# TensorE computes the two score pairs of an attention unit apart, with the unit's other matmuls between them

## The chip, the cores and the metric

The kernel runs on one core of one Trainium2 chip. Times are device microseconds (us) of one execution. The figure for a kernel is the median of several runs; the profile is one execution taken apart by the hardware profiler. TensorE does the matmuls and transposes, ScalarE the exponentials and the gelu, VectorE most copies out of PSUM and the normalisations, GpSimd the gathers and some subtractions, SyncE starts the plain DMAs.

## The reference: one layer of a small language model

A batch of 8 sequences of 1024 tokens, 192 channels wide. Token rows, segment rows and positions are added; then comes attention with 12 heads of 16 channels, then a quantised feed-forward block:

```python
h = tok_table[x] + seg_table[mask] + pos
a = layernorm(h)
q, k, v = split(a @ qkv_weight.T)              # 12 heads of 16 channels
q, k = layer_norm(q) * 16 ** -0.5, layer_norm(k)
h = h + (softmax(q @ k.T) @ v) @ proj_weight.T
f = quantise(layernorm(h))
h = h + (quantise(clip(gelu(f @ w1.T + b1))) @ w2.T + b2)
```

The scores of one sequence are 12 x 1024 x 1024 numbers, each of which needs an exponential.

## The kernel before, in words

**Half-steps and units.** The work is cut into 16 half-steps, one for 512 queries of a sequence. A half-step has 24 units (`UNITS`): one unit is four heads (`GH`) by 128 keys by 512 queries. For a unit TensorE makes four score matmuls (`scores`, line 1212), each 64 rows deep and 512 columns wide, into the four PSUM banks of `ps_s`, one head a bank. Heads 0 and 1 are pair 0, heads 2 and 3 are pair 1; two heads of a pair lie in different halves of the rows. ScalarE takes each pair out with one exponential of 128x1024 into `probs` (`exps`, line 679). Later TensorE multiplies the probabilities with the values (`heads`, line 1232): four heads side by side in 32 columns each, fp32, which the profile shows as eight matmul records, summed in the one bank `ps_o` over the units of a group.

**Order on TensorE.** The order of every engine is written out by hand. `PLAN` (line 77) has one line per unit, `START_PLAN` (line 128) the same for half-step 0. A word is a job: `h` is one `heads`; A to I, X, Y and W are the other matmuls and transposes (A transposes the normed rows, B and C make q, k and v, D and E transpose q and k, F and G turn the attention output, H is the projection, I transposes the quantised rows, X and Y are the feed-forward matmuls, W turns the feed-forward weights and runs in half-step 1 alone). Small letters and N, P, R, S are VectorE work or copies that ScalarE makes. Jobs belong to other half-steps than the scores (`LAG`, line 175): those of A to E are for the half-step two ahead, so half-steps 14 and 15 have none of them.

`one` (line 1328) walks a half-step: for each unit first all four scores, then the jobs of that unit's line. `HEADS_BEHIND` (line 165) is 2: the n-th `h` of a half-step is the `heads` of unit n - 2. Counted through `PLAN` this means that unit 14's line makes `heads` of unit 13, unit 15's those of 14, unit 16's those of 15. Unit 0's line makes those of units 22 and 23 of the half-step before and unit 13's those of units 10, 11 and 12; in all others `heads` is two or three units behind. In half-step 0 `h` of units 1 to 6 is the `heads` of the unit just before.

The semaphores that matter here are these. Pair p of unit u is computed after pair p of unit u - 1 has been read by ScalarE, and `heads` of a unit waits for both exponentials of it:

```python
pe.wait_ge(exp_done, 2 * UNITS * s + (2 * u - 1 + j // 2))     # L1224, scores, at j = 0 and j = 2
pe.wait_ge(exp_done, 2 * UNITS * s + (2 * u + 2))              # L1245, heads
act.wait_ge(scores_mm, 2 * UNITS * s + (2 * u + pair + 1))     # L681, exps
```

The jobs use the three banks of `ps_j` in turn (X two of them, B the third), and wait at line 1259 for the copy of the bank's last user. On ScalarE the six gelus of a half-step (line 676) stand between the exponentials of unit 12 and unit 13, with a table load before and after them. X of block t waits for the gelu of block t - 2.

The lines of `PLAN` with what TensorE does in them, for half-steps from 2 on:

```
u0  h h          u6  h            u12 C0 B0 X0                    u18 h C2 D1
u1  Y0 Y1 Y2 F0 Y3 F1   u7  h     u13 X1 B1 X2 X3 B2 X4 X5 B3 h h h   u19 E1 h
u2  G0 F2 F3 H0 G1      u8  h I0  u14 h                           u20 D2 h
u3  h h          u9  I1 h A0      u15 h                           u21 h D3 E2
u4  G2 G3 H1 H2 H3      u10 I2 h A1 A2   u16 h                    u22 E3 h
u5  h h          u11 h A3 I3      u17 D0 E0 C1                    u23 C3 h
```

Of the kernel before, what the change touches and what calls it, by code (L numbers as in the profile page):

```python
# [27 lines left out]
X = mybir.AxisListType.X  # L28

P = 128  # L30
B, SEQ = 8, 1024
C = 192
H, D = 12, 16
# [11 lines left out]
GH = 4  # L45
# [4 lines left out]
UNITS = HG * TB  # L50
# [52 lines left out]


JOB_KINDS = "ABCDEFGHIWXY"


def words(plan, first_copy):

    taken, units = {"h": 0, "o": first_copy, "g": 0}, []  # L110
    for line in plan.strip("\n").split("\n"):
        units.append([])
        for word in line.split():
            if word in taken:
                units[-1].append((word, taken[word], 0))
                taken[word] += 1
            else:
                units[-1].append((word[0], int(word[1]), int(word[3:]) if word[2:] else None))
    return units


UNIT_WORK = words(PLAN, 0)
JOBS = [w[:2] for unit in UNIT_WORK for w in unit if w[0] in JOB_KINDS]
GELU_UNIT = next(u for u, unit in enumerate(UNIT_WORK) if ("g", 0, 0) in unit)
# [33 lines left out]
START_WORK = FIRST_WORK + [w for line in STEP0_WORK for w in line]  # L158
START_JOBS = [((k, t), s) for k, t, s in START_WORK if k in JOB_KINDS]

# [18 lines left out]
def unit_work(s0):  # L179
    return UNIT_WORK if s0 else STEP0_WORK  # L180


def passes(s0):

    return HG if s0 else 2 * HG


def copies_to(s0):

    return HG * s0 + (HG if s0 else 0)  # L190


def unit_tile(s0, u):

    per = UNITS // passes(s0)
    p, m = divmod(u, per)
    return p % HG, p // HG * per + m
# [34 lines left out]
def layer(nc, x_tok, x_seg, tok_table, seg_table, w_qkv, w_proj, w1, b1, aw1, aa1, w2, b2, aw2, aa2,  # L232
          pos, out):
    ctx = ExitStack()
    with ctx:
# [3 lines left out]
        def sem(name):  # L239
            return ctx.enter_context(nc.semaphore(name))  # L240
# [31 lines left out]
        def squares_at(half0, t):  # L272
# [83 lines left out]
        scores_mm, exp_done, heads_mm, heads_out = (  # L356
            sem(n) for n in ("scores_mm", "exp_done", "heads_mm", "heads_out"))
# [23 lines left out]
        def attends(s0):  # L381
            return 0 <= s0 < HALVES
# [347 lines left out]
        def _(dve):  # L730
# [254 lines left out]
            def split_weights():  # L985

                dve.wait_ge(scale_ready, 1)
                for n, ((dst, src), (high, _)) in enumerate(zip(weight_halves(wl), weight_halves(wh))):
                    if n in (0, 1, 3):
                        dve.wait_ge(high_weights, n + 1)  # L990
                        last = stt(out=dst, in0=src, scalar=w_scale[:], in1=high, op0=ALU.mult, op1=ALU.subtract)
                last.then_inc(weights_ready, 1)
# [167 lines left out]
        def _(pe):  # L1160
# [48 lines left out]
                pe.wait_ge(rows_added, 2)  # L1209
                pe.wait_ge(ones_written, 1)  # L1210

            def scores(s0, s, u):
                par, nh = s0 // 2 % 2, s0 % 2
                group, m = unit_tile(s0, u)
                if u == 0 and nh == 0:
                    pe.wait_ge(job_out["D"], (s + (2 if s0 else 1)) * TH)
                    pe.wait_ge(job_out["E"], (s + (2 if s0 else 1)) * TH)
                if s0 == 0 and u == UNITS // 2:
                    pe.wait_ge(job_out["D"], 2 * TH)
                    pe.wait_ge(job_out["E"], 2 * TH)  # L1220
                for j in range(GH):
                    if j % 2 == 0 and (u or attends(s0 - 1)):

                        pe.wait_ge(exp_done, 2 * UNITS * s + (2 * u - 1 + j // 2))  # L1224
                    head = GH * group + j
                    rows = slice(head % 2 * (P // 2), (head % 2 + 1) * (P // 2))
                    last = mm(ps_s[:, j], kT[rows, par, head // 2, m * P:(m + 1) * P],  # L1227
                              qT[rows, par, head // 2, nh * NQ:(nh + 1) * NQ], start=True, stop=True)
                    if j % 2:
                        last.then_inc(scores_mm, 1)  # L1230

            def heads(s0, s, u):
                par = s0 // 2 % 2
                group, m = unit_tile(s0, u)
                p, n = divmod(u, UNITS // passes(s0))
                if u == 0 and s0 % 2 == 0:

                    pe.wait_ge(job_out["C"], (s + (2 if s0 else 1)) * TH)
                if s0 == 0 and u == UNITS // 2:
                    pe.wait_ge(job_out["C"], 2 * TH)  # L1240
                if n == 0 and (p or attends(s0 - 1)):

                    pe.wait_ge(heads_out, copies_to(s0) + p)

                pe.wait_ge(exp_done, 2 * UNITS * s + (2 * u + 2))  # L1245
                for j in range(GH):
                    last = mm(ps_o[32 * j:32 * j + 2 * D, :], v_sb[:, par, m, (GH * group + j) * VE:(GH * group + j) * VE + 2 * D],  # L1247
                              probs[:, u % PROBS, j], start=(n == 0), stop=(n == UNITS // passes(s0) - 1))
                last.then_inc(heads_mm, 1)
# [78 lines left out]
            def one(s0, s, b):  # L1328
                for u in range(UNITS):
                    if attends(s0):  # L1330
                        scores(s0, s, u)
                    for kind, t, at in unit_work(s0)[u]:
                        if kind in job_mm:
                            job(s0 if at is None else at, s if at is None else at, kind, t)
                        elif kind == "h" and t >= HEADS_BEHIND and attends(s0):
                            heads(s0, s, t - HEADS_BEHIND)
                        elif kind == "h" and t < HEADS_BEHIND and attends(s0 - 1):

                            heads(s0 - 1, s - 1, UNITS + t - HEADS_BEHIND)

            def tail():
                for u in range(UNITS - HEADS_BEHIND, UNITS):
# [73 lines left out]
            for kind, t, s in FIRST_WORK:  # L1416
                if kind in JOB_KINDS:
                    job(s, s, kind, t)
            halfsteps(one)
            tail()  # L1420

# [34 lines left out]
```

## Time and profile before

| what | before |
|---|---|
| runs, median of 3 | 1069.84 us (1069.6 to 1072.44) |
| profiled execution, first to last instruction | 1067.6 us |
| a half-step in the middle, as the trace shows it | 61.6 us |
| TensorE busy | 979.4 us, 92% |
| ScalarE busy | 872.6 us, 82% |
| VectorE busy | 813.9 us, 76% |
| GpSimd busy | 411.8 us, 39% |

The profiled execution's own time is its span, 1067.6 us; the runs are timed from outside, and their median lies 2.2 us above it. A share is an average over the whole span: the half-steps repeat with a period, and within one the engines take turns at being the one that is waited for. In the rows, L1227 are the scores, L1247 the heads, L682 the exponentials.

### The profile page before, as it was taken

The numbers are of one execution on the slowest core, as the hardware profiler recorded it, in microseconds if no ns is written. First come the engines' busy times: TensorE is split into PE (matmuls) and PEld (weight loads), VectorE is DVE, ScalarE is ACT, GpSimd is POOL, SyncE is SP. The second block draws the span as 40 slices with busy tenths as digits, with TensorE's granted clock in tenths as the row PEclk, the third lists the DMA queues.
The fourth block names the chain that finished last, engine by engine and source line by source line (L and its number), as shares of the span: only waits on it lengthen the run. The fifth ranks groups of instructions, "written<-read, shape, count | busy, mean of one in ns | idle before, by whom it ended". The sixth has DMA issues, their size and how long they took to land.

```text
span 1067.6 us, 19577 instructions
## 1 busy us (share of the span) xinstructions
PE 979.4 (92%) x7571; PEld 389.1 (36%) x7571; DVE 813.9 (76%) x2325; ACT 872.6 (82%) x950; POOL 411.8 (39%) x345
## 2 busy tenths in 40 slices
PE   5589999999999999999999999999999999989885
PEld 4333433334342433434343343434334343413223
DVE  5878869788686969878696977869697886825347
ACT  1387788897979889797988979798888989798883
POOL 6555513635343353534435363443526412201000
PEclk9899999999999999999999999999999999999997
DMA  7511200303011040202102040110202000000000
GB/s 162 127 16 16 31 1 2 46 1 64 12 25 22 1 75 1 38 8 58 18 2 45 1 73 3 31 16 16 30 1 45 1 16 1 16 1 1 16 1 31
DMA packets 25762, 28.62 MB, mean 27 GB/s; under 512 B 5027, under 2 KB 22182, under 8 KB 25670
## 3 DMA queue, kind: packets, MB, share of 16 engines
q0 software_dynamic: 16896, 11.80, 9.4%
q1 hardware_dynamic: 8624, 15.55, 4.8%
q8 instruction: 61, 1.00, 0.4%
q14 instruction: 31, 0.25, 0.1%
q10 hardware_dynamic: 150, 0.01, 0.0%
HBM read 21.06 MB, written 6.29 MB: 26 GB/s over the span
## 4 chain that ended last, share of the span: by engine, by line
PE 40%; ACT 30%; DVE 24%; issue 3%; POOL 3%; DMA 0%
ACT probs L682 22%; PE ps_o L1247 12%; PE ps_s L1227 8%; PE ps_j L1271 4%; ACT gelu L676 4%; PE ps_j L1279 3%; PE ps_j L1325 3%; POOL stack L592 3%; PE ps_j L1286 2%; PE ps_j L1292 2%; ACT L676 2%; ACT L682 2%; DVE hn L797 2%; PE ps_j L1311 2%; PE ps_j L1296 2%
## 5 line engine op out<-in xcount | busy, mean ns | idle before, releaser
L682 ACT ACTIVATE probs<-ps_s 128x1024 f32<-128x1024 f32 x768 | 736.1, 1023 | 125.5 <-PE ps_s L1227 120.6
L1247 PE MATMUL ps_o<-probs,v_sb 128*32 128x512 f32 x3072 | 394.7, 605 | 0.2 <-DVE o_sb L859 0.2
L1227 PE MATMUL ps_s<-qT,kT 64*128 64x512 f16 x1536 | 264.3, 384 | 35.0 <-ACT probs L682 25.2
L592 POOL TENSOR_TENSOR stack<-sq,stack 128x384 f16<-128x384 f32 x124 | 120.5, 992 | 162.9 <-DVE stack L846 162.9
L1227 PEld LDWEIGHTS ps_s<-qT,kT 64*128 64x128 f16 x1536 | 61.5, 93 | 299.5 <-ACT probs L682 267.6
L525 POOL DMA_INDIRECT h_all<-in_L_tok_token_table,idx x60 | 96.7, 1611 | 59.5 <-DMA h_all<-in_L_tok_segm_table,idx 41.2
L1247 PEld LDWEIGHTS ps_o<-probs,v_sb 128*32 128x32 f32 x3072 | 69.1, 109 | 124.3 <-issue 116.1
L601 POOL TENSOR_TENSOR y_sb<-y_sb,b_row 128x768 f32<-128x768 f32 x14 | 25.4, 1814 | 198.8 <-DVE y_sb L931 198.8
L581 POOL TENSOR_TENSOR sq<-qk 128x384 f32<-128x384 f32 x56 | 46.2, 826 | 139.5 <-DVE qk L894 139.5
L525 POOL DMA_INDIRECT h_all<-in_L_tok_segm_table,idx x56 | 87.2, 1557 | 15.2 <-issue 13.1
L1279 PE MATMUL ps_j<-wh,partsT 128*128 128x384 f16 (+1 forms) x384 | 71.5, 296 | 1.0 <-ACT partsT L663 0.7
L1286 PE MATMUL ps_j<-ident_h,stack 128*128 128x128 f16 x768 | 61.2, 224 | 11.8 <-POOL stack L592 10.4
L676 ACT ACTIVATE gelu<-ps_j,b_sb,s_sb 128x512 f32<-128x512 f32 x90 | 65.3, 773 | 7.5 <-PE ps_j L1311 6.7
L894 DVE TENSOR_SCALAR qk<-ps_j,w_back 128x384 f32<-128x384 f32 x56 | 34.6, 618 | 48.1 <-PE ps_j L1279 48.0
L1286 PEld LDWEIGHTS ps_j<-ident_h,stack 128*128 128x128 f16 x768 | 45.6, 100 | 50.1 <-issue 39.3
L859 DVE COPY o_sb<-ps_o 128x512 f32<-128x512 f32 x47 | 32.0, 680 | 41.4 <-PE ps_o L1247 41.4
L846 DVE CAST stack<-sq 128x384 f16<-128x384 f32 x128 | 58.7, 500 | 2.2
L878 DVE TENSOR_SCALAR gelu<-gelu,ia,qlo 128x512 f32<-128x512 f32 x90 | 58.4, 648 | 0.0
L1311 PE MATMUL ps_j<-xqT,w1T 96*128 96x512 bf16 x180 | 52.9, 388 | 3.7 <-ACT gelu L676 2.7
L1279 PE MATMUL ps_j<-wl,partsT 128*128 128x192 f16 (+1 forms) x256 | 54.3, 295 | 0.0
L879 DVE TENSOR_SCALAR gelu<-gelu,qhi 128x512 f32<-128x512 f32 x90 | 50.8, 565 | 3.2
L1271 PE MATMUL ps_j<-wpT,oT 96*128 96x192 f32 x240 | 45.7, 333 | 0.0
(201 smaller groups left out, 1118.5 us busy)
## 6 DMA issues: line engine op xcount, KB each, us to landing
out<-h_all SPq DMA_DIRECT2D x15, 384.0 KB
h_all<-in_positions SPq DMA_DIRECT2D x7, 768.0 KB
gelu<-in_L_ffn_w SPq DMA_DIRECT2D x2, 576.0 KB
h_all<-in_L_tok_token_table,idx POOLq DMA_INDIRECT x60
h_all<-in_L_tok_segm_table,idx POOLq DMA_INDIRECT x56
probs<-in_L_attn_qkv_weight SPq DMA_DIRECT2D x2, 432.0 KB, 4.7
h_all<-in_positions SPq DMA_DIRECT2D x2, 384.0 KB, 8.0
o_nat<-in_L_ffn_alpha_a SPq DMA_DIRECT2D x1, 384.0 KB
```

The source lines that it names most:

```text
L525: nc.gpsimd.indirect_dma_start(out=h_tile(half, j), out_offset=None, in_=table, in_offset=bass.IndirectOffsetOnAxis(ap=idx[:, which, t:t + ...
L592: last = nc.gpsimd.tensor_tensor(low, src, high, ALU.subtract)
L676: nc.scalar.activation(gelu[:, j], bank(("X", j), s0), ACT.Gelu, bias=b1_sb[:, j:j + 1], scale=s1_sb[:, j:j + 1]).then_inc(job_out["X"], 1)
L682: nc.scalar.activation(probs[:, u % PROBS, 2 * pair:2 * pair + 2], ps_s[:, 2 * pair:2 * pair + 2], ACT.Exp, scale=SCORE_SCALE).then_inc(ex ...
L846: last = nc.vector.tensor_copy(high, src)
L878: link(ts(gelu[:, t], gelu[:, t], ia2[:], qlo[:], ALU.mult, ALU.max))
L1227: last = mm(ps_s[:, j], kT[rows, par, head // 2, m * P:(m + 1) * P], qT[rows, par, head // 2, nh * NQ:(nh + 1) * NQ], start=True, stop=True)
L1247: last = mm(ps_o[32 * j:32 * j + 2 * D, :], v_sb[:, par, m, (GH * group + j) * VE:(GH * group + j) * VE + 2 * D], probs[:, u % PROBS, j], ...
L1271: last = mm(ps[:, 0:C], oT[:, t, k], wpT[:, k], start=(k == 0), stop=(k == 1))
L1279: last = mm(ps[:, 0:hi - lo], partsT[:, t, m], w, start=(n == 0), stop=(n == len(passes) - 1))
L1286: last = nc.tensor.transpose(bank16((kind, t), s0, F16)[:, i * P:(i + 1) * P], src, ident_h[:])
L1311: last = mm(ps, w1T[:, k, t * P:(t + 1) * P], xqT[:, k], start=(k == 0), stop=(k == 1))
```

## The change

`scores` gets one pair at a time. `one` computes pair 0 at the start of a unit as before, and pair 1 where the unit's other TensorE work is half done by a table of costs in nanoseconds (`PE_NS`). The cut never comes ahead of the unit's first job; where there is only one job, pair 1 comes behind it, at the unit's end. The table counts W in every half-step, though W runs in one. ScalarE's order, all waits' values and the order of the jobs are left as they are.

```diff
+PE_NS = {"h": 816, "A": 168, "B": 810, "C": 415, "D": 336, "E": 336, "F": 327, "G": 218, "H": 652, "I": 150,
+         "X": 432, "Y": 498, "W": 350}
...
-            def scores(s0, s, u):
+            def scores(s0, s, u, pair):
...
-                for j in range(GH):
-                    if j % 2 == 0 and (u or attends(s0 - 1)):
-                        pe.wait_ge(exp_done, 2 * UNITS * s + (2 * u - 1 + j // 2))
+                if u or attends(s0 - 1):
+                    pe.wait_ge(exp_done, 2 * UNITS * s + (2 * u - 1 + pair))
+                for j in (2 * pair, 2 * pair + 1):
...
             def one(s0, s, b):
                 for u in range(UNITS):
                     if attends(s0):
-                        scores(s0, s, u)
+                        scores(s0, s, u, 0)
+                    done, middle = 0, sum(PE_NS.get(w[0], 0) for w in unit_work(s0)[u]) / 2
+                    split = attends(s0)
                     for kind, t, at in unit_work(s0)[u]:
+                        cost = PE_NS.get(kind, 0)
+                        if split and cost and done and done + cost / 2 > middle:
+                            scores(s0, s, u, 1)
+                            split = False
+                        done += cost
...
+                    if split:
+                        scores(s0, s, u, 1)
```

Worked through for `PLAN`, with `|` where pair 1 now stands: `h | h` in units 0, 3 and 5; `Y0 Y1 Y2 | F0 Y3 F1`, `G0 F2 F3 | H0 G1` and `G2 G3 | H1 H2 H3` in units 1, 2 and 4; `| h` in units 6 and 7, where the table counts a W ahead of the cut that does not run; `h | I0`, `I1 h | A0`, `I2 h | A1 A2`, `h | A3 I3` in 8 to 11; `C0 B0 | X0` in 12; `X1 B1 X2 X3 B2 X4 | X5 B3 h h h` in 13; `h |` in 14, 15 and 16; `D0 E0 | C1` in 17; and in 18 to 23 one cut each between an `h` and the jobs beside it.

## Rows read from the trace of the kernel before

**Rows 1.** The page's first part: span, and busy time and share of each engine

```profile
span 1067.6 us, 19577 instructions
...
PE 979.4 (92%) x7571; PEld 389.1 (36%) x7571; DVE 813.9 (76%) x2325; ACT 872.6 (82%) x950; POOL 411.8 (39%) x345
```

**Rows 2.** Waits: who waited for whom, us in total, times, longest

```profile
ACT probs L682 <- PE ps_s L1227: 120.6, 183, 2.7
...
PE ps_s L1227 <- ACT probs L682: 25.2, 68, 0.5
```

**Rows 3.** Stretches: one half-step, busy us of each engine, granted clock, DMA

```profile
242.13:303.73 61.60, 58.90 (x472) 22.85 (x468) 49.72 (x140) 52.93 (x57) 27.10 (x22) 1.00 0.17 33
```

**Rows 4.** Timeline of TensorE: start, us, work [idle before]; units 5 to 9

```profile
502.27 0.61 PE L1227 MATMUL ps_s<-qT,kT 64*128 64x512 f16 x4
502.80 1.93 PE L1247 MATMUL ps_o<-probs,v_sb 128*32 128x512 f32 x16
504.66 0.61 PE L1227 MATMUL ps_s<-qT,kT 64*128 64x512 f16 x4
...
507.09 0.39 PE L1227 MATMUL ps_s<-qT,kT 64*128 64x512 f16 x2 [0.50 <-ACT probs L682]
507.40 1.06 PE L1247 MATMUL ps_o<-probs,v_sb 128*32 128x512 f32 x8
508.40 0.91 PE L1227 MATMUL ps_s<-qT,kT 64*128 64x512 f16 x4
...
512.83 0.33 PE L1299 MATMUL ps_j<-ident_h,parts 128*128 128x128 f16 x3 [0.37 <-DVE parts L801]
```

**Rows 5.** Timeline of ScalarE: two runs of exponentials, the last two gelus

```profile
505.09 7.76 ACT L682 ACTIVATE probs<-ps_s 128x1024 f32<-128x1024 f32 x8 [0.46 <-PE ps_s L1227]
...
524.37 1.45 ACT L676 ACTIVATE gelu<-ps_j,b_sb,s_sb 128x512 f32<-128x512 f32 x2 [0.47 <-PE ps_j L1311]
...
527.13 11.45 ACT L682 ACTIVATE probs<-ps_s 128x1024 f32<-128x1024 f32 x12
```

**Rows 6.** Timeline of TensorE, units 0 and 1: transposes F, matmuls Y, scores

```profile
554.50 0.49 PE L1292 MATMUL ps_j<-ident,o_sb 128*128 128x128 f32 x3
554.83 0.66 PE L1325 MATMUL ps_j<-w2T,hq 128*128 128x192 bf16 x6
555.32 0.49 PE L1292 MATMUL ps_j<-ident,o_sb 128*128 128x128 f32 x3
555.75 0.61 PE L1227 MATMUL ps_s<-qT,kT 64*128 64x512 f16 x4
```

**Rows 7.** Timeline of TensorE, units 18 and 20: scores with a wait inside

```profile
536.21 0.79 PE L1227 MATMUL ps_s<-qT,kT 64*128 64x512 f16 x4
...
540.91 0.84 PE L1227 MATMUL ps_s<-qT,kT 64*128 64x512 f16 x4
```

**Rows 8.** Timeline of TensorE, units 12 to 14

```profile
518.21 0.42 PE L1279 MATMUL ps_j<-wh,partsT 128*128 128x192 f16 x3
...
519.45 0.60 PE L1311 MATMUL ps_j<-xqT,w1T 96*128 96x512 bf16 x2
...
529.12 0.39 PE L1227 MATMUL ps_s<-qT,kT 64*128 64x512 f16 x2 [0.49 <-ACT probs L682]
```

**Rows 9.** Timeline, single instructions: two exponentials, and a score's weight load that waited

```profile
502.70 1.02 ACT L682 ACTIVATE probs<-ps_s 128x1024 f32<-128x1024 f32 x1 [1.17 <-PE ps_s L1227]
...
507.82 1.04 ACT L682 ACTIVATE probs<-ps_s 128x1024 f32<-128x1024 f32 x1
...
508.92 0.10 PEld L1227 LDWEIGHTS ps_s<-qT,kT 64*128 64x128 f16 x2 [0.42 <-ACT probs L682]
```

**Rows 10.** Timeline of TensorE in half-step 0, units 3 and 4

```profile
69.96 0.83 PE L1286 MATMUL ps_j<-ident_h,stack 128*128 128x128 f16 x12 [0.32 <-POOL stack L592]
70.72 0.60 PE L1227 MATMUL ps_s<-qT,kT 64*128 64x512 f16 x4
```

More of the change, by code:

```diff
@@ L1210, in start @@
                 pe.wait_ge(ones_written, 1)
-            def scores(s0, s, u):
+            def scores(s0, s, u, pair):
                 par, nh = s0 // 2 % 2, s0 % 2
                 group, m = unit_tile(s0, u)
-                if u == 0 and nh == 0:
+                if u == 0 and nh == 0 and pair == 0:
                     pe.wait_ge(job_out["D"], (s + (2 if s0 else 1)) * TH)
                     pe.wait_ge(job_out["E"], (s + (2 if s0 else 1)) * TH)
-                if s0 == 0 and u == UNITS // 2:
+                if s0 == 0 and u == UNITS // 2 and pair == 0:
                     pe.wait_ge(job_out["D"], 2 * TH)
                     pe.wait_ge(job_out["E"], 2 * TH)
-                for j in range(GH):
-                    if j % 2 == 0 and (u or attends(s0 - 1)):
-                        pe.wait_ge(exp_done, 2 * UNITS * s + (2 * u - 1 + j // 2))
+                if u or attends(s0 - 1):
+                    pe.wait_ge(exp_done, 2 * UNITS * s + (2 * u - 1 + pair))
+                for j in (2 * pair, 2 * pair + 1):
                     head = GH * group + j
```

## The prediction, on record before the changed kernel was run

> **What bounds the kernel now.** The page's first part comes first: TensorE is busy 92% of 1067.6 us, ScalarE 82% [rows 1]. Neither is full, so the next view is who waits for whom: ScalarE stood 120.6 us waiting for scores, TensorE only 25.2 us for ScalarE to free a score bank [rows 2]. The stretches then show that half-steps repeat: 61.60 us each, 58.90 of it TensorE, 52.93 ScalarE, the granted clock at 1.00 (2.4 GHz), DMA at 0.17 [rows 3]. TensorE has 2.7 us of idle time in a half-step by that row. Nothing that only moves work on TensorE can bring more than about that.
>
> Inside a half-step the two engines take turns, which the timelines show. ScalarE runs without a gap through 8 exponentials from unit 6 on and through 12 from unit 13 to 18 [rows 5]; in those stretches TensorE stops 0.50 us ahead of a pair [rows 4] and 0.49 us (unit 14) [rows 8], and these stops cost nothing. From unit 18 round to unit 5 it is TensorE that works without a gap, and ScalarE that waits for scores [rows 2]. So three prices are needed: what a cut costs TensorE, what it wins there, and whether ScalarE still gets its scores in time where ScalarE sets the end.
>
> **What a cut costs.** Starts of consecutive TensorE work give the time that work holds the engine. Four scores hold it 502.80 - 502.27 = 0.53 us, two hold it 507.40 - 507.09 = 0.31 [rows 4]. Two times 0.31 is 0.62, so leaving a score group costs about 0.10 (0.09 by these rounded starts). One `heads` holds it 508.40 - 507.40 = 1.00, two in a row 504.66 - 502.80 = 1.86 [rows 4]: leaving heads costs 0.14. Three transposes F before a Y, which uses the array in the same way, hold it 554.83 - 554.50 = 0.33; three before scores 555.75 - 555.32 = 0.43 [rows 6]: leaving full-array work for scores costs 0.10. The scores themselves (64 rows) and the heads (32 columns) each use the array in another way, and every change of it has this price.
>
> A cut adds a score group. Between two `h` it adds leaving heads and leaving scores, 0.24. Between two full-array jobs it adds 0.10 + 0.10 = 0.20. Between an `h` and a full-array job a change was there already, and it adds 0.10. Where pair 1 stands at a unit's end it joins pair 0 of the next unit, and nothing is added; in units 6 and 7 it stays beside pair 0.
>
> The Trainium skill (TensorEngine Tiling, Key Properties) says that changing the tiling mode drains TensorE, which agrees with these 0.10 to 0.14 us. Its page TensorE: Matmul & The Clock Gate (Single matmul latency) gives a warm constant of 398 cycles, 0.166 us, for one matmul that hides nothing. By that figure, the eighteen changes added in units 18 to 5 would come to an estimated 3.0 us, not the 1.9 below, and the forecast to about 1135. The rows were taken in this kernel and decide.
>
> **Units 18 to 5, where TensorE sets the end.** Six cuts beside an `h` (units 18 to 23): 6 x 0.10 = 0.60. Three between two `h` (0, 3, 5): 0.72. Three between full jobs (1, 2, 4): 0.60. Sum 1.92. What the cuts win is the waits inside the score groups of units 18, 20 and 23, which take 0.79 and 0.84 (unit 23 as 20) against 0.61 undisturbed [rows 4, 7]: 0.18 + 0.23 + 0.23 = 0.64, as pair 1 now comes a job later. Net **+1.28**. Bounds: the cuts cost nothing and the waits go, -0.64; every one of the twelve costs 0.24 and no wait goes, +2.88. I take the rows' value in the middle, since all prices stand in this stretch. Waits of D for GpSimd's stack stay as they are: that chain begins at C1 and E1 on TensorE, and moves with them.
>
> **Units 14 to 16, the new wait.** Here the line is a single `h`, so pair 1 comes behind it, and that `h` is the `heads` of the unit just before, which waits for both its exponentials. Before, pair 1 waited for the same exponential and was computed first, so ScalarE had its next work a `heads` earlier. Now there is a loop that nothing overlaps: `heads` of u - 1, then pair 1 of u, then its exponential, then `heads` of u. Its length: heads 1.00 [rows 4]; start of scores to start of the exponential 502.70 - 502.27 = 0.43 [rows 4, 9]; the exponential 1.02 [rows 9]; its end to the next TensorE work 508.92 - (507.82 + 1.04) = 0.06 [rows 9]. Together 2.51. Before, ScalarE set 11.45 / 12 x 2 = 1.91 a unit there [rows 5]. So +0.60 a unit, three units, **+1.80**. Behind the waiting `heads` stand pair 1 of the unit, pair 0 of the next and all else of TensorE; ScalarE, for which this was a gapless stretch, waits for pair 1. Bounds: 0 if ScalarE is so far behind that the scores still lie ready; it can't be, as the loop is longer than the two exponentials beside it. Above, 2.51 against the 1.54 that scores and heads need alone, 3 x 0.97 = 2.9.
>
> **Units 6 to 13 and 17.** In 6 to 11 ScalarE and VectorE's rows set the end: A0 waits 0.37 for `parts` [rows 4], whose chain runs through VectorE. The four cuts (0.40) fall into TensorE's own stops, 0.50 and 0.30 (the 0.91 against 0.61) and that 0.37 [rows 4]: 0. If the cover is gone they cost 0.4. In unit 12 pair 1 moves behind C0 and B0, 519.45 - 518.21 = 1.24 us later [rows 8], its exponential perhaps 0.5 later, and with it the gelus; ScalarE gets that back at its 0.47 wait for the last two X [rows 5], which come earlier. X of blocks 2 and 3, though, wait for gelus 0 and 1 and may push B3 and three heads back: 0 to +1.0. In unit 17, D0 and E0 (0.7) now run beside the exponential that pair 1 waits for, which wins up to 0.5. I set both against each other: 0.
>
> **The sum.** 1.28 + 1.80 = 3.08 a half-step; 15 half-steps (1 to 15) make 46. In half-step 0 the loop is in units 1 to 6: in 1, 2, 5 and 6 at the same 0.60, taking the 1.91 [rows 5] for these too, 2.4; in 3 and 4 the jobs D and E fill it: scores 0.53, heads 1.00 and 70.72 - 69.96 = 0.76 make 2.29 [rows 4, 10], so 0.2 each; 2.8 in all, its other cuts against its other waits. Together +49 on 1067.6, or, as the median lies 2.2 above the span, 1069.84 + 49 = **1119 us**.
>
> **Rivals.**
> *The waits go and the cuts are covered.* Place: the 25.2 us that TensorE idles ahead of scores [rows 2]. ScalarE's work comes evenly, no pair 1 is waited for, and every change of array mode hides under weight loads. Time: at best 1069.84 - 25 = 1045. It decides if a change costs under 0.64 / 18 = 0.036 us and the heads in units 14 to 16 find their exponentials done. Against it: 0.10 and 0.14 are read in stretches without waits, and line 1245 makes the loop certain. Chance 0.06.
>
> *The cuts cost, the loop doesn't.* If the last exponentials of units 13 to 15 are long done when heads comes, 1.28 x 16 = 20: 1090. For it: three heads in unit 13 give ScalarE 2.72 us (1.86 for two and 0.86 for one more) [rows 4]. Against: ScalarE was the late one there, with a 0.49 stop of TensorE [rows 8]. Chance 0.08.
>
> *The gelu stretch isn't cancelled.* +1.0 a half-step more, with 3.08: 4.1 x 15 + 2.8 = 64, 1134. For it, X waits for gelus and these for unit 12's exponential. Chance 0.18.
>
> *Nothing moves.* Units 6 and 7 aren't changed and 14 to 16 hold one job; if the rest balanced, 1070. Chance 0.03.
>
> **How the numbers follow.** The forecast, with its bounds near its middle, has 0.65. The low end, 1091, lies at the case without the loop; with waits won, cuts free and only the loop it is (1.80 - 0.64) x 15 + 2.8 = 20, the same. The high end, 1139, takes the gelu case and a little of the upper bounds. A measurement can tell 0.3%, about 3 us, from no change. Faster 0.06, same 0.03, slower 0.91.
>
> **What would show it.** In the changed profile: heads of units 14 to 16 preceded by idle time of about 0.9 us on TensorE, released by L682; units 14, 15 and 16 starting 2.5 us apart; exponentials there in ones with gaps of 0.6, not 12 in a row; score groups of two with 0.31 to the next start, and one `heads` at 1.00 each in units 0, 3 and 5; busy time of TensorE up by 20 to 40 us, that of ScalarE unchanged; units 18 to 5 longer by 1.3. I would be wrong if half-steps stay at 61.6 or fall, if heads start at once in units 15 and 16, or if scores in the middle of a unit hold TensorE only 0.22.

## The result, and the profile after

The changed kernel takes 1116.62 us (median of 4 runs, 1115.32 to 1120.02) against 1069.89 for the kernel before beside it: ratio 1.0434, 95% interval 1.0412 to 1.0455. It is 4.3% slower, 46.7 us; the forecast was 1119, slower by 49. The profiled execution spans 1113.6 us, 46.0 more than before.

The page's first part, after:

```profile
span 1113.6 us, 19577 instructions
...
PE 1003.0 (90%) x7571; PEld 391.6 (35%) x7571; DVE 806.8 (72%) x2325; ACT 890.1 (80%) x950; POOL 413.1 (37%) x345
```

The instructions are the same 19577, but TensorE is busy 23.6 us longer and yet has a smaller share than in [rows 1]: the same matmuls hold it longer, and it also waits more. ScalarE's 17.5 us are no more work: there are as many exponentials, 1.02 us long on average as before. Those that follow one another without a gap overlap a little in the records (0.92 us from start to start), and fewer do so now.

Waits, after (who waited for whom, us, times, longest):

```profile
ACT probs L686 <- PE ps_s L1231: 138.8, 315, 1.4
...
PE ps_o L1251 <- ACT probs L686: 34.1, 48, 0.9
...
PE ps_j L1315 <- ACT gelu L680: 17.4, 16, 2.1
...
PE ps_s L1231 <- ACT probs L686: 15.5, 29, 0.9
```

TensorE's wait ahead of scores fell from 25.2 [rows 2] to 15.5, which is what the cuts were to win. In its place stand 34.1 us of heads (L1251) waiting for exponentials, 48 times, about three in a half-step, and 17.4 us of X waiting for gelus. ScalarE waits for scores 138.8 us, more than the 120.6 before.

Timeline of TensorE, after, units 14 to 17 of half-step 7 (the stretch of the new loop):

```profile
548.44 0.39 PE L1231 MATMUL ps_s<-qT,kT 64*128 64x512 f16 x2
549.10 1.07 PE L1251 MATMUL ps_o<-probs,v_sb 128*32 128x512 f32 x8 [0.27 <-ACT probs L686]
550.10 0.60 PE L1231 MATMUL ps_s<-qT,kT 64*128 64x512 f16 x4
551.61 1.06 PE L1251 MATMUL ps_o<-probs,v_sb 128*32 128x512 f32 x8 [0.90 <-ACT probs L686]
552.61 0.61 PE L1231 MATMUL ps_s<-qT,kT 64*128 64x512 f16 x4
554.11 1.06 PE L1251 MATMUL ps_o<-probs,v_sb 128*32 128x512 f32 x8 [0.90 <-ACT probs L686]
555.11 0.60 PE L1231 MATMUL ps_s<-qT,kT 64*128 64x512 f16 x4
```

Heads now start 551.61 - 549.10 = 2.51 and 554.11 - 551.61 = 2.50 us apart, the second and third behind an idle 0.90 (the first, unit 14's, behind 0.27): the loop, at the predicted length of 2.51. The four score matmuls after it are pair 1 of one unit and pair 0 of the next. ScalarE over the same time:

```profile
547.11 2.86 ACT L686 ACTIVATE probs<-ps_s 128x1024 f32<-128x1024 f32 x3
550.53 1.94 ACT L686 ACTIVATE probs<-ps_s 128x1024 f32<-128x1024 f32 x2 [0.56 <-PE ps_s L1231]
553.04 1.94 ACT L686 ACTIVATE probs<-ps_s 128x1024 f32<-128x1024 f32 x2 [0.57 <-PE ps_s L1231]
555.54 2.86 ACT L686 ACTIVATE probs<-ps_s 128x1024 f32<-128x1024 f32 x3 [0.57 <-PE ps_s L1231]
```

Where 12 exponentials ran without a gap [rows 5], pairs of them now stand 0.56 us apart.

In the timelines of both kernels a unit's length is the time from its pair 0 to that of the next. Summed over stretches, mean of half-steps 3 to 11, in us:

```
                    units 0-5   6-11   12-13   14-17   18-23   half-step
before                 16.17   12.60   10.99    7.97   13.86       61.60
after                  17.53   12.27   12.10    9.10   13.31       64.30
difference             +1.36   -0.34   +1.10   +1.13   -0.55       +2.70
```

Half-steps 2 to 12 grow by about 2.7 each, half-step 0 by 1.9 (55.07 to 56.95), and 14, which has none of the jobs A to E, by 4.9 (57.97 to 62.86); together with 1, 13 and 15 that makes the 46.0. The 4.9 are 1.61 in units 12 and 13, 1.70 in 14 to 17, 0.40 in 18 to 23, which give nothing back there, and 1.18 in the rest.

### The profile page after: what moved, and what is told of

It is laid out like the page before. It is cut to its first block, busy times and chain, and to the rows that moved or that the text cites. A ratio compares the mean times of both kernels' runs of the same rounds, so it can differ in the third digit from the quotient of the medians.

```text
span 1113.6 us, 19577 instructions
## 1 busy us (share of the span) xinstructions
PE 1003.0 (90%) x7571; PEld 391.6 (35%) x7571; DVE 806.8 (72%) x2325; ACT 890.1 (80%) x950; POOL 413.1 (37%) x345
## 4 chain that ended last, share of the span: by engine, by line
PE 72%; ACT 20%; DVE 6%; issue 2%; DMA 0%
PE ps_o L1251 28%; PE ps_s L1231 18%; ACT probs L686 14%; PE ps_j L1283 5%; PE ps_j L1275 4%; PE ps_j L1290 3%; ACT gelu L680 3%; PE ps_j L1329 3%; PE ps_j L1315 2%; PE ps_j L1296 2%; ACT L680 2%; ACT L686 2%; PE ps_j L1300 2%; PE ps_j L1303 1%; PE ps_j L1309 1%
## 5 line engine op out<-in xcount | busy, mean ns | idle before, releaser
L686 ACT ACTIVATE probs<-ps_s 128x1024 f32<-128x1024 f32 x768 | 752.0, 1024 | 152.0 <-PE ps_s L1231 138.8
L1251 PE MATMUL ps_o<-probs,v_sb 128*32 128x512 f32 x3072 | 404.5, 606 | 34.4 <-ACT probs L686 34.1
L1231 PE MATMUL ps_s<-qT,kT 64*128 64x512 f16 x1536 | 287.9, 386 | 18.1 <-ACT probs L686 15.5
L1231 PEld LDWEIGHTS ps_s<-qT,kT 64*128 64x128 f16 x1536 | 69.8, 93 | 380.9 <-ACT probs L686 230.0
L596 POOL TENSOR_TENSOR stack<-sq,stack 128x384 f16<-128x384 f32 x124 | 120.6, 992 | 163.5 <-DVE stack L850 163.5
L1251 PEld LDWEIGHTS ps_o<-probs,v_sb 128*32 128x32 f32 x3072 | 64.1, 108 | 143.9 <-ACT probs L686 72.9
L1315 PE MATMUL ps_j<-xqT,w1T 96*128 96x512 bf16 x180 | 56.4, 397 | 18.3 <-ACT gelu L680 17.4
L882 DVE TENSOR_SCALAR gelu<-gelu,ia,qlo 128x512 f32<-128x512 f32 x90 | 53.2, 591 | 0.0
```

The costliest lines, as they stand in the source:

```text
L596: last = nc.gpsimd.tensor_tensor(low, src, high, ALU.subtract)
L686: nc.scalar.activation(probs[:, u % PROBS, 2 * pair:2 * pair + 2], ps_s[:, 2 * pair:2 * pair + 2], ACT.Exp, scale=SCORE_SCALE).then_inc(ex ...
L882: link(ts(gelu[:, t], gelu[:, t], ia2[:], qlo[:], ALU.mult, ALU.max))
L1315: last = mm(ps, w1T[:, k, t * P:(t + 1) * P], xqT[:, k], start=(k == 0), stop=(k == 1))
```

## The experiments

The first two take out, or do alone, the loop of units 14 to 16.

**Pair 1 ahead of the heads it would wait with**, in the changed kernel:

```diff
                         elif kind == "h" and t >= HEADS_BEHIND and attends(s0):
+                            if split and t - HEADS_BEHIND == u - 1:
+                                scores(s0, s, u, 1)
+                                split = False
                             heads(s0, s, t - HEADS_BEHIND)
```

> The changed kernel, but pair 1 goes ahead of a heads that belongs to the unit just before (units 14, 15, 16; in half-step 0 units 1 to 6), as in the kernel before; all other cuts stay. Theory (the loop heads, pair 1, exponential is a price of its own): the changed trace gives units 14 to 17 9.10 us where they took 7.97, so 1.13 x 15 comes back, and some 2.8 in half-step 0: about 1097 us, at most 1087 if all of 0.60 x 3 a unit comes back; heads of units 14 to 16 start without idle time, and the exponentials run in a row. Rival (the cuts' own array changes make the loss, the loop only fills time that the late gelus leave): 1112 to 1117 us.

Measured 1108.2 us, ratio 1.0356 (1.0341 to 1.0371): 8.4 us below the changed kernel, between the two expectations. The unit lengths show why. Units 14 to 17 take 8.12 us, so the loop is gone (-0.98 against the changed kernel), but units 18 to 23 take 13.94 instead of 13.31 (+0.63). The timeline of TensorE of this kernel, units 17 and 20:

```profile
552.74 0.83 PE L1290 MATMUL ps_j<-ident_h,stack 128*128 128x128 f16 x12 [0.40 <-POOL stack L596]
...
559.88 0.49 PE L1290 MATMUL ps_j<-ident_h,stack 128*128 128x128 f16 x6 [0.50 <-POOL stack L596]
```

TensorE arrives sooner and waits for GpSimd's `stack` instead; over the run this wait is 20.3 us here and 7.9 in the changed kernel. Part of the loop's time was spent while VectorE and GpSimd prepared D.

**The loop alone**, on the kernel before. In this run, and in those below that cut named units alone, `split` is taken back outside these units, as here:

```diff
                     split = attends(s0)
+                    if split and not (14 <= u <= 16 if s0 else 1 <= u <= 6):
+                        scores(s0, s, u, 1)
+                        split = False
```

> The kernel before with only the units 14 to 16 (half-step 0: 1 to 6) changed, where pair 1 goes behind the single heads; no array change is added. Theory (loop): units 15 and 16 take 2.51 us, half-steps grow by 1.3 to 1.9 us, 1092 to 1102 us in all. Rival (array changes alone cost): 1070 us, as nothing is cut. Rival (the loop's time comes back in units 18 to 23, where TensorE waits for exponentials): 1074 to 1080 us.

Measured 1097.02 us, ratio 1.0252 (1.0237 to 1.0267). No change of array mode is added, and 27 us are lost. Timeline of TensorE, units 15 to 17:

```profile
541.65 1.06 PE L1251 MATMUL ps_o<-probs,v_sb 128*32 128x512 f32 x8 [0.90 <-ACT probs L686]
542.65 0.60 PE L1231 MATMUL ps_s<-qT,kT 64*128 64x512 f16 x4
544.15 1.07 PE L1251 MATMUL ps_o<-probs,v_sb 128*32 128x512 f32 x8 [0.90 <-ACT probs L686]
545.15 0.61 PE L1231 MATMUL ps_s<-qT,kT 64*128 64x512 f16 x4
546.66 0.39 PE L1231 MATMUL ps_s<-qT,kT 64*128 64x512 f16 x2 [0.91 <-ACT probs L686]
546.99 0.84 PE L1290 MATMUL ps_j<-ident_h,stack 128*128 128x128 f16 x12
```

Units 14 to 17 are 1.94 longer, 0.41 comes back in 18 to 23. The last two rows also show what unit 17's own cut is worth: here both its pairs stand ahead of D0 and E0, and TensorE idles 0.91 us; in the changed kernel D0 and E0 run in that time, and unit 17 takes 2.20 us instead of 2.79. That is 0.59 of the difference between the loop's 1.94 in these units here and its 0.98 beside the cut of unit 17. The rest is that without the loop the cut unit 17 is itself longer, 2.39 against 2.03 in the kernel before, as D0 then waits for `stack` (the first row of the run above).

**Cuts in units 0 to 5 alone** (`s0 and u <= 5`):

> The kernel before with only units 0 to 5 cut as in the changed kernel (half-steps 1 to 15). Theory (each cut costs its array changes, 0.24 between two heads and 0.20 between full-array jobs, and nothing absorbs it): units 0 to 5 1.32 to 1.36 us longer, half-steps too, 1090 us. Rival (absorbed at the waits of units 7 to 12): units 0 to 5 longer by the same, half-steps by 0.5 to 0.9, 1077 to 1083 us. Rival (an even stream of scores wins as much): 1070 us.

Measured 1085.03 us, ratio 1.0150 (1.0135 to 1.0165). Units 0 to 5 are 1.36 longer, to the hundredth as in the changed kernel; then 0.43 comes back in units 6 to 11, so the half-step is 0.87 longer, as in the first rival, though the time lies 2 us above that rival's range. What gives way is the wait of A0 for VectorE's `parts`. In the kernel before it is 0.34 to 0.47 us in each of half-steps 1 to 12 (0.37 in [rows 4]); here TensorE comes later and A0 starts at once:

```profile
518.19 0.34 PE L1303 MATMUL ps_j<-ident_h,parts 128*128 128x128 f16 x3
```

Twelve changes of array mode cost 1.36 / 12 = 0.11 us each. Unit 2 has only 0.12 of it, because its cut fills a wait of H0 for VectorE's copy of G0. This is the weight load of H0 in the kernel before:

```profile
557.28 0.62 PEld L1271 LDWEIGHTS ps_j<-wpT,oT 96*128 96x128 f32 x4 [0.16 <-DVE oT L896]
```

The other five units are 0.24 to 0.26 longer each, 0.12 to 0.13 a change. The estimate from the Trainium skill (TensorE: Matmul & The Clock Gate, Single matmul latency), 0.166 each or 2.0 for the twelve, is too high here. The Trainium skill (TensorEngine Tiling (Array Packing), Key Properties) also states that changing the tiling mode drains TensorE; a price at every change agrees with that, but no run shows the drain itself.

Timeline of TensorE in the changed kernel, units 5 and 6, `h | h`:

```profile
521.48 0.39 PE L1231 MATMUL ps_s<-qT,kT 64*128 64x512 f16 x2
521.80 1.06 PE L1251 MATMUL ps_o<-probs,v_sb 128*32 128x512 f32 x8
522.80 0.39 PE L1231 MATMUL ps_s<-qT,kT 64*128 64x512 f16 x2
523.12 1.06 PE L1251 MATMUL ps_o<-probs,v_sb 128*32 128x512 f32 x8
524.12 0.61 PE L1231 MATMUL ps_s<-qT,kT 64*128 64x512 f16 x4
```

The unit takes 524.12 - 521.48 = 2.64; in [rows 4] it was 504.66 - 502.27 = 2.39. TensorE idles nowhere in it: the 0.25 is the two added changes. The weight loads of the first `heads` begin with its first matmul, at 521.80, and not ahead of it:

```profile
521.80 0.16 PEld L1251 LDWEIGHTS ps_o<-probs,v_sb 128*32 128x32 f32 x8 [0.23 <-issue]
```

So the price of a change may be a drain, or a weight load that nothing hides; these runs don't tell the two apart, and the sum needs only the price.

**Cuts in units 18 to 23 alone** (`s0 and u >= 18`):

> The kernel before with only units 18 to 23 cut (half-steps 1 to 15). Theory (a cut beside a heads costs 0.10, and the waits inside the score groups of 18, 20 and 23, 0.64, go): 0 to 0.55 us a half-step won, 1062 to 1070 us. Rival (the cuts cost 0.10 each and the waits only move): 0.6 us a half-step lost, 1079 us. In the two last half-steps these units have no other jobs than heads, so nothing is won there.

Measured 1075.46 us, ratio 1.0047 (1.0035 to 1.0059): 0.23 lost in these units, neither of the two. The waits for exponentials in units 18 and 20 do go, and others come. Timeline of this kernel, a weight load and a matmul of TensorE:

```profile
541.98 0.34 PEld L1290 LDWEIGHTS ps_j<-ident_h,stack 128*128 128x128 f16 x6 [0.28 <-DVE kT L900]
...
545.40 0.49 PE L1290 MATMUL ps_j<-ident_h,stack 128*128 128x128 f16 x6 [0.51 <-POOL stack L596]
```

D1 waits 0.28 for the copy of E0 out of the same bank (0.20 before). D2 waits for GpSimd's subtraction, 0.51 where it had been 0.16 in the kernel before:

```profile
541.91 0.49 PE L1286 MATMUL ps_j<-ident_h,stack 128*128 128x128 f16 x6 [0.16 <-POOL stack L592]
```

Unit 23 alone wins what was forecast (0.13). In units 18 and 20, what had looked like ScalarE's doing in [rows 7] was hiding VectorE's and GpSimd's chain.

**Cuts in unit 12 alone, and in unit 13 alone** (`s0 and u == 12`; `s0 and u == 13`):

> The kernel before with unit 12 alone cut (half-steps 1 to 15): pair 1 behind C0 and B0. Theory (its exponential starts some 0.5 us later, the table load and all gelus move by that, X of blocks 2 and 3 wait for gelus 0 and 1, and the rest of unit 13 on TensorE moves too): units 12 and 13 together 0.4 to 0.7 longer, 1076 to 1080 us. Rival, as the prediction had it (ScalarE gets it back at its 0.47 wait ahead of the fifth gelu): 1070 us, and that wait is gone.

> The kernel before with unit 13 alone cut (half-steps 1 to 15): pair 1 between X4 and X5, behind the waits of X for gelus 0 and 1. Theory (the 0.31 us of pair 1 and a change of 0.20 move from ahead of those waits, where they cost nothing, to behind them): unit 13 0.4 to 0.55 longer; at unit 14 ScalarE has some 0.4 us of work in hand, so 0 to 0.5 of it counts: 1070 to 1078 us. Rival (units 12 and 13 cost only together): 1070 us.

Measured 1079.90 us (ratio 1.0087, 1.0071 to 1.0102) and 1077.46 us (1.0064, 1.0049 to 1.0080). With unit 12 cut, units 12 and 13 are 0.70 longer and nothing comes back. ScalarE in that kernel, the late exponential, and the wait that should have given the time back:

```profile
524.00 1.02 ACT L686 ACTIVATE probs<-ps_s 128x1024 f32<-128x1024 f32 x1 [0.63 <-PE ps_s L1231]
...
529.73 0.78 ACT L680 ACTIVATE gelu<-ps_j,b_sb,s_sb 128x512 f32<-128x512 f32 x1 [0.47 <-PE ps_j L1315]
```

The 0.47 ahead of the fifth gelu is there unchanged: X of block 4 comes after those of blocks 2 and 3, which wait for the late gelus, so the whole row moves. With unit 13 cut, pair 1 stands behind these waits instead of ahead of them: 0.40 there, 0.22 less in 14 to 17, 0.21 more in 18 to 23, as B3 is late. Alone the two lose 0.74 and 0.47 a half-step.

**Neither the loop nor the cuts of 12 and 13; and those cuts undone with the loop kept:**

> The changed kernel without its cuts in units 12 and 13 and without pair 1 behind the heads of the unit just before (units 14 to 16); the other cuts stay. Theory (loop and gelu stretch each cost over 1 us and hide one another, so that undoing one alone brings little): what is left is the array changes, 0.88 and 0.26 a half-step as measured alone, 1085 to 1090 us. Rival (the loop was the lesser part for good, the rest is cuts): 1100 us or more.

> The changed kernel without its cuts in units 12 and 13; the loop of units 14 to 16 stays. It fills the table of loop and gelu cuts: neither 1094.3, gelu cuts only 1108.2, both 1116.6. Theory (the loop runs while VectorE and GpSimd still prepare D1 and D2 from B3, so part of it is hidden; the cuts in 12 and 13 move B3 itself): the loop adds 1.2 to 1.6 a half-step to the 1094.3, 1112 to 1118 us, so that beside the loop the gelu cuts are worth almost nothing. Rival (both add up, each 8 to 14): 1102 to 1104 us.

Measured 1094.26 us (ratio 1.0228, 1.0213 to 1.0244) and 1105.47 us (1.0330, 1.0313 to 1.0346). The first is above its expected range: the other cuts cost more than the runs of units 0 to 5 and 18 to 23 say. The second lies below the range of the theory that loop and gelu stretch hide one another, and 1.5 us above that of its rival; it refutes the theory:

```
us                        no loop    loop    the loop adds
no cuts in 12 and 13       1094.3  1105.5        11.2
cuts in 12 and 13          1108.2  1116.6         8.4
```

They nearly add up. The loop is worth 8 to 11 us beside the other cuts and 27 alone. Beside them, without the cuts in 12 and 13, it adds 1.19 in units 14 to 17 (9.31 against 8.12) and gives 0.64 back in 18 to 23 (13.31 against 13.95): what hides it are unit 17's cut and the waits for VectorE and GpSimd.

**Cuts in units 8 to 11 alone** (`s0 and 8 <= u <= 11`):

> The kernel before with units 8 to 11 alone cut (half-steps 1 to 15). Theory as predicted (TensorE's stops and the wait of A0 cover the four cuts): 1070 us, the half-step within 0.1. Rival (in units 10 and 11, behind A0, nothing covers them; the run without loop and gelu cuts had 0.3 more from unit 10 to 12): 0.2 to 0.4 a half-step, 1073 to 1076 us.

Measured 1076.01 us, ratio 1.0058 (1.0043 to 1.0073): 0.31 in units 6 to 11, 0.17 in 12 and 13. Timeline of TensorE, A0 in unit 9 and pair 1 of unit 12:

```profile
516.21 0.33 PE L1303 MATMUL ps_j<-ident_h,parts 128*128 128x128 f16 x3 [0.60 <-DVE parts L805]
...
521.70 0.39 PE L1231 MATMUL ps_s<-qT,kT 64*128 64x512 f16 x2 [0.41 <-ACT probs L686]
```

Up to A0 nothing is lost (its wait for `parts` rises from 0.37 to 0.60, as TensorE comes sooner). Behind it nothing covers the cuts. The same 0.21 in unit 12 stands in the run without loop and gelu cuts, and is part of what was missing there; unit 17, whose cut no run takes alone, is 0.15 longer in that run too.

**Heads joined**, an attempt to use the price of a change the other way round, on the kernel before:

```diff
-E1 n3 h
-D2 h x1
+E1 n3
+D2 h h x1
...
-E3 x3 x4 h
-x5 C3 h
+E3 x3 x4
+x5 C3 h h
```

> The kernel before, whole scores and no cut, but the heads of unit 19's line joined to those of unit 20 and that of unit 22 to 23: two changes of array mode fewer in a half-step. Theory (leaving heads costs 0.14, and these units are set by TensorE): 0.28 a half-step less, 1065.5 us; if VectorE's and GpSimd's chain sets units 18 to 20, only 0.14, 1067.5 us. Rival (ScalarE loses its lead as scores come later after two heads): 1070 us or more.

Measured 1094.84 us, ratio 1.0232 (1.0218 to 1.0246): 25 us slower instead of 2 to 4 faster. ScalarE and TensorE in units 20 and 21:

```profile
550.40 0.39 PE L1227 MATMUL ps_s<-qT,kT 64*128 64x512 f16 x2 [0.46 <-ACT probs L682]
...
551.31 0.39 PE L1227 MATMUL ps_s<-qT,kT 64*128 64x512 f16 x2 [0.52 <-ACT probs L682]
...
552.28 1.92 PE L1247 MATMUL ps_o<-probs,v_sb 128*32 128x512 f32 x16
554.14 0.60 PE L1227 MATMUL ps_s<-qT,kT 64*128 64x512 f16 x4
554.57 1.94 ACT L682 ACTIVATE probs<-ps_s 128x1024 f32<-128x1024 f32 x2 [1.47 <-PE ps_s L1227]
```

Behind the light unit 19 TensorE waits for two exponentials in turn, 0.98 us, and behind the two heads of the heavy unit 20 ScalarE waits 1.47 for scores. The banks hold the scores of one unit, so a light unit can't pay for a heavy one. No version tried beats the kernel before.

## Why the prediction was right, and where its steps were not

The time, 1116.6, lies 2.4 below the forecast and inside the range. The two main mechanisms, the price of a change and the loop, are there, but that the total came so close is partly luck, as several terms were wrong in opposite directions. Point by point:

**What a cut costs: right.** 1.32 was summed for units 0 to 5 (0.72 + 0.60), 1.36 measured, in the changed kernel and alone. The three cuts between full-array jobs were each summed at 0.20: units 1 and 4 cost 0.26, and unit 2 only 0.12, as there TensorE was not without a wait. That 0.43 of the 1.36 comes back in units 6 to 11 was not in the sum.

**The loop: right in its length, too large in its worth.** 2.51 us were predicted and measured, at 0.90 idle. The sum gave it +1.80 a half-step; in place units 14 to 17 grew by 1.13. Two things were left out or set aside: TensorE comes to unit 14 after a longer unit 13, with most of the exponentials done (0.27 us of wait are left), so this unit is 0.3 shorter; and D0 and E0 run beside the last turn of the loop, which the prediction had as "up to 0.5" and then cancelled.

**The waits won in units 18, 20 and 23: the wrong step, with a small effect.** The term -0.64 took the waits inside the score groups as ScalarE's alone. Alone the cuts there lose 0.23 instead of winning 0.04, since E0's copy and GpSimd's `stack` are next. In the changed kernel these units are 0.55 shorter all the same: TensorE is late through the loop, and finds everything ready. Of the loop and the gelu cuts it is the loop that does this: with it and without the gelu cuts these units take the same 13.31, with the gelu cuts and without it 13.94. "Waits of D for GpSimd's stack stay as they are" was wrong; they fell, from 10.4 us in all to 7.9. Units 18 to 5 together are 0.81 longer where 1.28 were summed.

**Units 12, 13 and 17 set to zero: wrong.** "ScalarE gets that back at its 0.47 wait" fails, as that wait hangs on the same gelus. Units 12 and 13 cost 1.10 (unit 12 alone 0.70, unit 13 alone 0.40). This was the rival with 0.18, and its mechanism was there. Its time, 1134, didn't come, because units 14 to 17, 18 to 23 and 6 to 11 came out 0.67, 0.51 and 0.34 below the sum.

**Units 6 to 11 at no cost: right up to A0**, wrong behind it (0.18 and 0.10 in units 10 and 11 alone, and 0.2 in unit 12).

So the sum of 3.08 a half-step stands against 2.70 through errors that offset: +1.10 not counted in units 12 and 13, against 0.67 less in units 14 to 17, 0.51 less in 18 to 23 and 0.34 in 6 to 11.

Nor are the half-steps alike, as the sum took them. Half-step 14 lost 4.9 where the sum had 3.08. Half-step 0 lost 1.9 where 2.8 were forecast, and not by the loop as forecast: the loop alone adds 1.1 there, and the two runs that undo it beside the other cuts take 57.75 and 57.83 us for it, more than the changed kernel's 56.95. There unit 10 takes 5.98 us against 4.37; why is open.

The rival of a faster kernel falls by the loop run and that of units 0 to 5: TensorE's stops had cost little, and each change of array mode has its price.

## What to carry to other kernels

Where one engine makes work for a second, and waits for it again, write down the loop that remains when nothing overlaps (here heads, scores, exponential: 2.51 us) before moving a producer behind a consumer; it must be shorter than the slower engine's own time for a unit, here 1.91. A producer's stop in a stretch that the other engine sets need not be a reserve (it covered the cuts of units 8 and 9, but in units 14 to 16 ScalarE had to wait), and a wait that goes shows the next engine's wait behind it: look for what is ready only just later. Changes of TensorE's tile shape cost 0.10 to 0.14 us each here, so work of one shape is best kept together, but in the one try here not at the price of units of unequal length.

## What the runs showed that was not expected

Costs of parts didn't add up: the loop is worth 27 us alone and 8 to 11 beside the other cuts, while the cuts of units 12 and 13, worth 7 to 10 us each alone, are worth 11 to 14 together in the changed kernel. And joining two `heads`, in two places of a half-step, which takes away a change of array mode worth 0.14 us each time, cost 25 us in all. Why units 6 to 11 in the changed kernel and with only units 0 to 5 cut come out shorter by 0.34 and 0.43 was read from the lengths and the wait for `parts`, which is gone from nearly all half-steps of both; no run moved that chain by itself.
